# Recurrent layer pair on one core: tail over two chunk times, fewer spread banks, more product banks

## The reference, cut to what matters

```python
xn = layernorm(x)
s = mamba_block(xn)              # below
g = silu(fp4_down(silu(fp4_gate(xn)) * fp4_up(xn)))   # blockwise 4-bit quantised inputs and weights
x = x + s * g
xn = layernorm(x)
s = attention(xn)                # 16 heads of 16, over the 2 sequences at each token
g = silu(three blocks of h + linear(gelu(layernorm(linear(h)))))   # with bias; low rank part folded into weights
x = x + s * g

def mamba_block(x):
    u = layernorm(x) * g1 + b1
    xi, z = u @ in_proj          # 512 each
    xc = silu(causal_conv(xi, 4 taps per channel) + conv_b)
    dt, Bm, Cm = split(xc @ x_proj)
    dt = softplus(dt @ dt_proj + b)
    h[t] = exp(dt[t] * A) * h[t-1] + dt[t] * Bm[t] * xc[t]     # 512 channels x 16 states
    y[t] = sum over states of h[t] * Cm[t], plus D * xc[t]
    x = x + (y * silu(z)) @ out_proj
    return x + gelu(layernorm(x) @ w1 + b1) @ w2 + b2
```

## Time and profile before

| | us |
|---|---|
| median of 3 runs | 2985.43 |
| lowest, highest | 2978.42, 2988.9 |
| the profiled execution | 2981.44 |
| its span | 2979.3 |
| mean granted clock of PE, of full speed | 0.782 |

### The profile page before, as it was taken

How to read it: one execution, slowest core, us unless ns; L and a number is a source line. 1 busy time by engine, 2 the same in 40 slices (tenths; PEclk the granted TensorE clock), 3 DMA queues, 4 the chain that set the end, 5 groups by cost and what they waited for, 6 DMA issues and landing times.

```text
span 2979.3 us, 28883 instructions
## 1 busy us (share of the span) xinstructions
PE 1925.2 (65%) x7760; PEld 1465.3 (49%) x7760; DVE 1937.7 (65%) x2306; ACT 1486.6 (50%) x2992; POOL 1526.0 (51%) x1329
## 2 busy tenths in 40 slices
PE   0555857577685757667575776857667575765766
PEld 0333646455464545546454554645455464544644
DVE  2367767766676776667677666766666676766642
ACT  0255646446463544646464474645547364654532
POOL 1167555656355565536556463655556364555431
PEclk9956878778787878877787787878778786877877
DMA  5000000000000000000000000000000000000000
GB/s 143 4 11 1 1 1 11 1 12 1 11 1 0 12 1 11 1 12 1 1 11 1 12 1 11 1 0 12 0 11 1 12 1 0 11 1 8 1 8 4
DMA packets 31524, 25.55 MB, mean 9 GB/s; under 512 B 12038, under 2 KB 30278, under 8 KB 31318
## 3 DMA queue, kind: packets, MB, share of 16 engines
q1 hardware_dynamic: 31318, 23.23, 2.8%
HBM read 19.03 MB, written 4.19 MB: 8 GB/s over the span
## 4 chain that ended last, share of the span: by engine, by line
PE 23%; POOL 21%; issue 19%; ACT 19%; DVE 12%; POOLq 1%; ACTq 1%; DVEq 0%; DMA 0%
PE bank L488 9%; POOL drive L905 5%; ACT decay L723 4%; ACT L723 4%; PE bank L481 3%; DVE drive L1030 3%; PE bank L647 3%; POOL xd L1003 3%; PE bank L519 2%; POOL t_sm L929 2%; POOL wide L1008 2%; DVE dt L1221 2%; PE bank L603 2%; PE bank L537 1%; POOL drive L904 1%
## 5 line engine op out<-in xcount | busy, mean ns | idle before, releaser
L1030 DVE TENSOR_TENSOR_SCAN drive<-decay,drive 128x1032 f32<-128x1032 f32 x256 | 606.0, 2367 | 278.4 <-POOL drive L905 259.7
L905 POOL TENSOR_TENSOR drive<-wx,bc_sb 128x1024 f32<-128x1024 f32 x256 | 614.7, 2401 | 0.0
L904 POOL TENSOR_TENSOR drive<-carry,zero 128x8 f32<-128x8 f32 x256 | 124.9, 488 | 862.0 <-ACT carry L732 784.8
L655 PE MATMUL y_ps<-ident,decay 128*128 128x128 f32 x2048 | 353.8, 330 | 285.1 <-DVE decay L1035 279.3
L655 PEld LDWEIGHTS y_ps<-ident,decay 128*128 128x128 f32 x2048 | 307.6, 174 | 340.7 <-DVE decay L1035 292.8
L723 ACT ACTIVATE decay<-dt,aneg 128x256 f32<-128x256 f32 x1024 | 435.3, 499 | 1.5
L1035 DVE TENSOR_TENSOR decay<-drive,bc_ps 128x1024 f32<-128x1024 f32 x256 | 312.5, 1221 | 8.8
L664 PE MATMUL bc_ps<-bc,pick 64*128 64x256 f32 x512 | 157.2, 395 | 159.2 <-DVE decay L1035 159.1
L488 PE MATMUL bank<-w_l,op_b 128*128 128x256 f32 x384 | 177.2, 642 | 77.3 <-ACT op_b L813 45.7
L664 PEld LDWEIGHTS bc_ps<-bc,pick 64*128 64x128 f32 x512 | 96.9, 236 | 218.2 <-DVE decay L1035 167.4
L927 POOL TENSOR_TENSOR t_sm<-t_mv,epsc 128x2 f32<-128x2 f32 x80 | 49.3, 617 | 269.9 <-DVE t_mv L1046 269.9
(11 more groups left out here) (199 smaller groups left out, 4380.4 us busy)
## 6 DMA issues: line engine op xcount, KB each, us to landing
x_t<-in_L_attn_x_dram SPq DMA_DIRECT2D x16, 256.0 KB, 2.9
x<-in_L_attn_x_dram SPq DMA_DIRECT2D x16, 256.0 KB, 2.9
out_dram<-s SPq DMA_DIRECT2D x16, 256.0 KB, 2.2
w_f<-in_L_attn_ffn_w_dram SPq DMA_DIRECT2D x2, 1024.0 KB
q_raw<-in_L_ffn_qweights_dram SPq DMA_DIRECT2D x1, 1536.0 KB
w_in<-in_L_attn_in_proj_w_dram SPq DMA_DIRECT2D x1, 1024.0 KB
b_l<-in_L_ffn_biases_dram SPq DMA_DIRECT2D x1, 768.0 KB
qkv_raw<-attn_in_proj_weight_dram SPq DMA_DIRECT2D x1, 768.0 KB
```

The source lines that it names most:

```text
L655: last = t.matmul(y_ps[j][:, g * P:(g + 1) * P], src(g, j), ident[:, :], start=(first and g == 0), stop=stop, is_transpose=True, skip_grou ...
L904: g_.tensor_tensor(d[:, :, 0], carry[:, n, :], zero8[:, :], ALU.add).then_inc(S["drive_ready"], 1)
L905: g_.tensor_tensor(d[:, :, 1:SEG].rearrange("p (g b) t -> p g b t", b=B), wx[par][:, :, :].rearrange("p g (b t) -> p g b t", b=B), bc_sb[n ...
L1030: v.tensor_tensor_scan(drv[:, :, :].rearrange("p s t -> p (s t)"), dec[:, :, :].rearrange("p s t -> p (s t)"), drv[:, :, :].rearrange("p s ...
```

## The change

- The tail is cut in A (out_proj and ffn) and B (attention, first block, first half of the second) for chunk c-1, and C (the rest) for chunk c-2. `x1` and `h` are doubled. There is one more period at the end.
- M now holds all quantised work of chunk c; its input is quantised at the end of the period before, and it has its own operand `xq_t`.
- Two banks `bc_ps` for the spread of B and C, four `bank` for dense products, in one order over all periods (`ORDER`, `BANK`, `EARLIER`). A product waits for the reader of the product four before it.
- ACT copies B and C to `bc_sb`, and h*C reads C from there. The copy of n waits for h*C of n-2; the spread of n waits for the copy of n-2 and no longer for an h*C.
- The convolution is made by PE: weights times each tap (`w_tap`, made in the preparation) on shifted columns of `u_t`, which keeps the last three columns of the chunk before; ACT's silu reads PSUM.
- y is summed by two products of 512 columns with the identity as weights, channels on partitions; D*x is a product with a diagonal. y needs no transposing before out_proj, and z is made with channels on partitions.
- Biases are one more product from rows of `b_rows` or `b_qkv` into the same bank.
- A tail norm is: DVE statistics and an add, one POOL power (`root`), two DVE passes in a later slot (`norm_apply`); three of them read PSUM.
- The loop is gone: every period is written out by the program that builds the kernel, and waits are for constants.

```diff
+USES = {
+    "A": [("op", "dve"), ("u2T", "act")] + [(f"f1{_m}", "act") for _m in range(4)] + [("f2", "dve")],
+    "B": [("xn1T", "act"), ("b0a", "dve"), ("qkv0", "dve"), ("qkv1", "dve"), ("qkv2", "act"), ("qkv3", "act"),
+          ("b0T", "act"), ("b0b", "dve"), ("ctxT", "act"), ("h1T", "act"), ("ao", "dve"), ("b1a", "dve")],
+    "C": [("b1T", "act"), ("b1b", "dve"), ("h2T", "act"), ("b2a", "dve"), ("b2T", "act"), ("b2b", "dve")],
+    "F": [("uT", "act"), ("xi0", "act"), ("xi1", "act"), ("z0", "act"), ("z1", "act"), ("xp", "dve"),
+          ("dt0", "act"), ("dt1", "act")],
+    "M": [("xqT", "act")] + [(f"{_n}{_j}{_h}", "act" if _n == "g" else "dve")
+                             for _j in range(2) for _n in "gu" for _h in range(2)]
+         + [(f"hqT{_k}", "act") for _k in range(3)] + [("dn", "act")],
+}
+OWN = {"A": -1, "B": -1, "C": -2, "M": 0, "F": 1}
+NBANK = 4
+NSPREAD = 2
+
+
+PE_SLOT = {
+    1: [("C", "b1T"), ("A", "op")],
+    2: [("M", "xqT"), ("C", "b1b")],
+    3: [("M", "g00"), ("M", "g01"), ("M", "u00"), ("M", "u01"), ("A", "u2T"), ("C", "h2T")],
+    4: [("M", "g10"), ("M", "g11"), ("M", "u10"), ("M", "u11"), ("A", "f10"), ("A", "f11"), ("C", "b2a")],
+    5: [("A", "f12"), ("A", "f13"), ("F", "uT")],
+    6: [("A", "f2"), ("C", "b2T"), ("F", "xi0")],
+    7: [("C", "b2b"), ("F", "xi1")],
+    8: [("F", "z0"), ("F", "z1")],
+    9: [("B", "xn1T"), ("F", "xp")],
+    10: [("B", "b0a"), ("B", "qkv0"), ("B", "qkv1"), ("B", "qkv2"), ("B", "qkv3"),
+         ("M", "hqT0"), ("M", "hqT1"), ("M", "hqT2")],
+    11: [("M", "dn"), ("F", "dt0"), ("F", "dt1")],
+    12: [("B", "b0T")],
+    13: [("B", "b0b")],
+    14: [("B", "ctxT"), ("B", "h1T")],
+    15: [("B", "ao"), ("B", "b1a")],
+}
+PERIODS = range(-1, NC + 2)
...
+ORDER = [(_c + OWN[_g], _g, _n) for _c in PERIODS for _s in range(NS) for _g, _n in PE_SLOT.get(_s, [])
+         if there(_c + OWN[_g])]
+BANK = {_key: _k % NBANK for _k, _key in enumerate(ORDER)}
+EARLIER = {_key: ORDER[_k - NBANK] for _k, _key in enumerate(ORDER) if _k >= NBANK}
...
+        y_ps = [ctx.enter_context(nc.psum_tensor(f"y_ps{j}", [P, 2 * TOK], F32)) for j in range(2)]
+        bc_ps = [ctx.enter_context(nc.psum_tensor(f"bc_ps{k}", [P, 2, TOK], F32)) for k in range(NSPREAD)]
         bank = [ctx.enter_context(nc.psum_tensor(f"bank{k}", [P, 512], F32)) for k in range(NBANK)]
...
+                (xi_raw[:, :, :], in_proj_w[:, 0:DI].rearrange("(k p) n -> p k n", p=P)),
+                (w_z[:, :, :], in_proj_w[:, DI:2 * DI].rearrange("(k p) n -> p k n", p=P)),
+                (cw_raw[:, :, :], conv_w.rearrange("d o t -> o d t").to_broadcast([P, DI, NTAP])),
...
+            def tokens(dst, lhs, rhs, kp, group, row=None):
 
                 for j in range(B):
                     for k in range(kp):
-                        last = t.matmul(dst[:, j * cols:(j + 1) * cols], lhs(k, j), rhs(k),
-                                        start=(k == 0 and j == 0), stop=(k == kp - 1), skip_group_check=True)
+                        last = t.matmul(dst[:, j * D:(j + 1) * D], lhs(k, j), rhs(k),
+                                        start=(k == 0 and j == 0), stop=(row is None and k == kp - 1),
+                                        skip_group_check=True)
+                if row is not None:
+                    last = t.matmul(dst[:, 0:B * D], ident[0:NROW, row:row + 1].to_broadcast([NROW, P]),
+                                    b_rows[:, None, :].to_broadcast([NROW, B, D]), start=False, stop=True,
+                                    skip_group_check=True)
                 last.then_inc(S["pe_" + group], 1)
...
+                elif name[:2] == "xi":
+                    m = int(name[2])
+                    pe.wait_ge(*emptied("F", fc, "uT"))
+                    for a in range(2):
+                        for tap in range(NTAP):
+                            for k in range(KD):
+                                last = t.matmul(dst[:, a * TOK:(a + 1) * TOK],
+                                                w_tap[:, tap, k, (2 * m + a) * P:(2 * m + a + 1) * P],
+                                                u_t[:, k, :, tap:tap + TC],
+                                                start=(k == 0 and tap == 0 and a == 0),
+                                                stop=(k == KD - 1 and tap == NTAP - 1), skip_group_check=True)
+                    last.then_inc(S["pe_F"], 1)
...
-            def sum_y(src, first, stop):
-
-                for j in range(B):
-                    for g in range(DG):
-                        last = t.matmul(y_ps[j][:, g * P:(g + 1) * P], src(g, j), ident[:, :],
-                                        start=(first and g == 0), stop=stop, is_transpose=True, skip_group_check=True)
+            def sum_y(hc, stop):
+
+                for m in range(2):
+                    last = t.matmul(y_ps[m][:, :], ident[:, :], hc[:, 4 * m:4 * m + 4, 1:SEG],
+                                    start=False, stop=stop, skip_group_check=True)
                 last.then_inc(S["y_summed"], 1)
 
-            def broadcast(chunk, par, n):
-
-                before = max(m for m in range(n - NS, n) if SPREAD[m % NS] == SPREAD[n])
-                pe.wait_ge(S["hc_done"], value(chunk, "hc_done", before + 1))
+            def skip_y():
+
+                for g in range(DG):
+                    last = t.matmul(y_ps[g // 2][:, (g % 2) * TOK:(g % 2 + 1) * TOK], d_diag[:, g, :], xc[:, g, :],
+                                    start=(g % 2 == 0), stop=False, skip_group_check=True)
+                last.then_inc(S["y_summed"], 1)
+
+            def broadcast(chunk, n):
+
+                pe.wait_ge(S["bc_sbuf"], value(chunk, "bc_sbuf", n - 1))
+                dst = spread(chunk, n)
                 for k, r in enumerate((n, NS + n)):
-                    last = t.matmul(bc_ps[SPREAD[n]][:, k, :], pick[:, r:r + 1].to_broadcast([64, P]), bc[par][:, :],
+                    last = t.matmul(dst[:, k, :], pick[:, r:r + 1].to_broadcast([64, P]), bc[chunk % 2][:, :],
                                     start=(k == 0), stop=True, skip_group_check=True)
                 last.then_inc(S["bc_spread"], 1)
...
+                act.wait_ge(S["hc_done"], value(chunk, "hc_done", n - 1))
+                a_.activation(bc_sb[n % 2][:, :, :], spread(chunk, n)[:, :, :], ACT.Copy).then_inc(S["bc_sbuf"], 1)
                 if n >= 4:
                     act.wait_ge(S["y_summed"], value(chunk, "y_summed", n - 2))
...
+                        act.wait_ge(S["u_saved"], value(fc - 1, "u_saved", 1))
+                        for k in range(KD):
+                            last = a_.activation(u_now[:, k, :, :],
+                                                 dense("F", fc, "uT")[:, k * TOK:(k + 1) * TOK]
+                                                 .rearrange("p (b t) -> p b t", b=B),
+                                                 ACT.Identity, scale=g1c[:, k:k + 1], bias=b1c[:, k:k + 1])
+                        last.then_inc(S["act_F"], 1)
+                    if s in (6, 7):
+                        m = s - 6
+                        act.wait_ge(*filled("F", fc, f"xi{m}"))
+                        two(lambda k: xc[:, 2 * m + k, :], dense("F", fc, f"xi{m}"), ACT.Silu, lambda k: 1.0,
+                            lambda k: cb[:, 2 * m + k:2 * m + k + 1], "F")
+                    if s == 8:
...
+            def root(name, of, chunk):
+
+                pool.wait_ge(S[of], value(chunk, of, 5))
+                g_.tensor_tensor(rstd[:, :], veps[:, :], mhalf[:, :], ALU.pow).then_inc(S[name], 1)
...
-                dve.wait_ge(S["bc_spread"], value(c, "bc_spread", n + 1))
                 v.tensor_tensor(dec[:, :, 1:SEG].rearrange("p (g b) t -> p g b t", b=B),
                                 drv[:, :, 1:SEG].rearrange("p (g b) t -> p g b t", b=B),
-                                bc_ps[SPREAD[n]][:, 1, :].rearrange("p (b t) -> p b t", b=B)[:, None, :, :]
+                                bc_sb[n % 2][:, 1, :].rearrange("p (b t) -> p b t", b=B)[:, None, :, :]
                                 .to_broadcast([P, DG, B, TC]), ALU.mult).then_inc(S["hc_done"], 1)
...
+            def norm_stats(src, name, chunk):
+
+                stats(src, t_st, t_mv, name, chunk)
+                dve.wait_ge(S[name], value(chunk, name, 4))
+                v.tensor_scalar(veps[:, :], t_mv[:, :, 1], EPS, None, ALU.add).then_inc(S[name], 1)
+
+            def norm_apply(dst, src, name, chunk, done):
+
+                dve.wait_ge(S[name], value(chunk, name, 1))
+                for j in range(B):
+                    last = v.tensor_scalar(dst[:, j, :], src[:, j, :], t_mv[:, j, 0:1], rstd[:, j:j + 1],
+                                           ALU.subtract, ALU.mult)
+                last.then_inc(S[done], 1)
...
+                if s == 1:
+                    dve.wait_ge(*filled("A", tc, "op"))
+                    dve.wait_ge(S["f_norm"], value(tc, "f_norm", 4))
```

(30 more changed lines are left out.)

## The result

The changed kernel takes 2996.53 us (median of 20 runs, 2983.18 to 3008.45) against 2983.63 (20 runs) for the kernel before: 1.0038 times as long, 95% interval 1.0025 to 1.0051. It is slower by a hair, where the prediction said 2755. The profiled execution has a span of 2995.4 us.

The account below looks back on a forecast made before the run. No engine is full, so waits set the time. Start 178, first chunk 128, second 151, thirteen of 157 (2041), last scanning period 140 and tail 115 make a span of 2753, plus 2: 2755 us; range 2555 to 3000.

Parts of the forecast that it names:

- The walk of 16 slots: Steady chunk, from h*C of state 3 onward, following what is late next through the queues: 157 us where 174 are now.
- warm paces for all of PE's work: PE in a steady chunk: work priced at high-clock times, 132 us after the change, four-matrix products at 1.8 us.
- Its own sign for the PE terms: PE: sum of y of 1.8 us, busy near 135 to 145 us a chunk, clock above 0.85.
- The second rival: PE's clock stays as it is: work in slots 3 to 11 takes 17 us more, 174 a chunk, about 2990; chance 0.08.
- The price of C in SBUF: h*C: +1.4 us in the five or six states after slot 12 that DVE and POOL bound, nothing elsewhere.
- The first rival: Turns of DVE and POOL at the port pair decide: 181 us a chunk, 3091 in all, slower; chance 0.15.
- attention and residual 3.1: Walk between h*C after state 13 and the three 1.22 us passes: attention and residual take 3.1 us.
- Engine sums: Busy time of a steady chunk: PE 132 us of warm work, DVE 110, POOL some 73, ACT near 98.
- Waits costed at nothing: ACT's copy waiting for h*C, the spread waiting for ACT's copy, SP's load order and the unrolled program: no cost.
- The waits only move: ACT, in order with 24 table loads, still holds up carries: 11 us more DVE idle, 168 a chunk, 2909; chance 0.11.
- The longest gaps: Sign for the walk: longest gaps between scans in slots 6 to 9 and 12 to 13.

Follow-up runs that it names:

- fill_qkv: Changed kernel with zero-weight filler products on PE in slot 10 alone, 3 before the third and 3 before the fourth qkv product: 2936.2 us (0.9837).
- keep_warm: Changed kernel with zero-weight filler products in front of PE's waits in seven places, 3 and 1 of them in slot 10: 2917.5 us (0.9761).
- psum33_warm: Changed kernel with C read from PSUM, three spread and three product banks, and zero-weight fillers before PE's waits: 2866.1 us (0.9579).
- no_pool_softplus: Changed kernel with POOL's two softplus passes of 1024 elements cut to 8 elements, values not the reference's: 2947.3 us (0.9874).
- szs_warm: Changed kernel with softplus Exp and Ln in slot 12, z products in slots 12 and 13, convolution silu a slot later, and fillers: 2766.0 us (0.9266).
- the three moves: Changed kernel with, each alone, softplus Exp and Ln in slot 12 (2903.8 us), convolution silu a slot later (2960.2), z products in slots 12 and 13 (2958.2).

## Why the prediction was wrong

The walk of 16 slots can be set beside the timelines, by the ends that it named (us; means of the thirteen steady chunks).

| stretch of the walk, ends with | walk | after | fill_qkv | keep_warm | psum33_warm | no_pool_softplus | szs_warm |
|---|---|---|---|---|---|---|---|
| h*C of state 5 | 20.0 | 18.4 | 18.4 | 18.4 | 19.4 | 18.4 | 18.4 |
| product xi1 | 31.0 | 31.7 | 31.7 | 31.7 | 31.7 | 31.7 | 31.7 |
| ACT's copy of xn1T | 14.6 | 13.0 | 13.0 | 13.0 | 12.6 | 13.0 | 8.3 |
| ACT's last copy of hqT | 15.4 | 21.4 | 18.5 | 20.1 | 22.1 | 21.4 | 19.2 |
| decay of state 13 | 19.0 | 20.8 | 19.8 | 19.9 | 19.6 | 20.8 | 15.1 |
| DVE's product wx | 16.0 | 20.1 | 20.1 | 20.1 | 19.5 | 17.1 | 20.1 |
| b1a statistics and copy | 13.0 | 16.0 | 16.3 | 13.8 | 13.8 | 15.8 | 13.8 |
| h*C of state 3 | 28.0 | 32.0 | 31.2 | 30.2 | 26.3 | 31.8 | 30.2 |
| chunk | 157 | 173.3 | 168.9 | 167.2 | 165.0 | 170.1 | 156.8 |

**The step that failed: warm paces for all of PE's work.** The walk's first three stretches, where PE is at 1.00, came out 2.5 us shorter than forecast. The other five are 18.8 us longer. In them PE waits, the clock falls, and its work is on the path. The fillers before all these waits (`keep_warm`) take 6.1 us off a steady chunk. If the larger gain of the two filler kernels is taken in each stretch (2.9, 1.0, 2.2 and 1.8 us in the fourth, fifth, seventh and eighth), it is 7.8; no one kernel has all of these. The prediction had 3.78 against 1.8 us for such a product in its own rows and a clock of 0.77, and still said that the busiest stretches are warm; they are, but it priced the idle ones warm too. Its own sign for the PE terms, a clock above 0.85, was met (0.855) and could not tell. The second rival, "the clock stays as it is", gave 174 a chunk and 2990 and had 0.08. Its time is nearly exact, but partly by luck: its mechanism is some two fifths of the miss, and it put the slow work in slots 3 to 11, where it was in 11 to 15 and 0. Its chance was too small. The range from 2555 to 3000 holds the measured time only by this rival's end of it.

**Turns.** The price of C in SBUF was near: +1.4 in five or six states, measured 6.3 us in five states of a steady chunk, and longest case 3.36. It is a mean of 0.3 to 2.1, and two of the five states are not after slot 12. The walk says that it holds these 7 to 8 us, but its terms show a turn plainly in state 15 alone (6.1); state 0 stands at 3.5 and took 5.6 (2.30 and 3.34). With fillers, C in PSUM takes 3.9 us off the eighth stretch and 0.6 off the sixth, so a part of the price is in the miss; which part, the terms don't tell. The first rival (181 a chunk, with 7 us in which neither DVE nor POOL works) is refuted: both are idle together for 33 us a chunk, and by taking C out of SBUF 78 us are gained, not 240. The rule cited ("SBUF — State Buffer", "Who interferes with whom" in the Trainium skill) agrees with these lines: with C in PSUM no h*C took over 1.222 us.

The walk also had every scan at 2.31 us. In the changed kernel those of states 3, 6, 8, 10, 12 and 13 took 2.75 to 3.41 as a mean, each begun beside a pass of POOL: 42.2 us a chunk for all sixteen, 37.8 before. And it left out that short steps with two SBUF inputs wait as long as large ones: "attention and residual 3.1" has a step of 0.18 us that took 2.37 and one that took 2.04. POOL's softplus passes are 3.0 of the 4.1 us by which that stretch is over: 0.75 through the scan, 2.2 through the first of these steps. Another 8 us of the 18.8 no run takes apart. C in SBUF, bank waits of the qkv products, the long scan of state 10 and further short turns (the add of two elements) lie there. That these are all of it is not shown.

**Engine sums.** PE: 147.2 us a chunk at a clock of 0.85, just over the 135 to 145 that were given; the four passes of a sum of y follow each other by 0.43 us, 1.72 (1.8 forecast), xi 13.8 for 64 passes (14.3). DVE 122.2, not 110: 6.3 of it are longer h*C and 4.4 longer scans; the rest wasn't taken apart. POOL 86, not 73: its five powers take 9.7 us a chunk where 5.7 were forecast, and six small passes (front norm and attention) 10.8 where the same ones took 2.7 before. ACT 95.3 (98 forecast, though 92.0 and the terms given make 95.5 or less), with 24 table loads as counted. DVE idles for 52 us, not 30; the forecast's own 157 less 110 would have been 47.

**Waits costed at nothing.** ACT's copy waits for h*C of two states before for 20.6 us a chunk; the price of this wait by itself wasn't measured. The spread, also costed at nothing, waits for ACT's copy of two states before once, for 2.9 us, in slot 12. Not only qkv3 waits for a bank: qkv2 does too, for 1.33 us, and these two small waits cost the 60 us that the fillers of slot 10 bring. What the unrolled program brought by itself no run shows: the thirteen steady chunks take 173.3 us each where they took 174.1. The start took 8 and the first chunk 8 us more than forecast, the second 14. With C in PSUM the first chunk took 126.7 us, with three and three banks and C in SBUF 138.0.

**"The waits only move"** (fourth rival, 168 a chunk, ACT holds up the carries) names a part as well. Its figure is near the 170 us of several kernels above, and moving ACT's steps in its queue gains 185 us of 2996 together with z. But these waits were in the walk, near their size (19.0 forecast, 20.8 measured for the stretch with softplus). They are what could be improved, not what was missed. The longest gaps were said to lie in slots 6 to 9 and 12 to 13. Slots 7, 8, 12 and 13 are among the longest; 11 (17.1) and 4 (14.0) were missed, and 6 and 9 (9.5 and 6.1) are short.

With C in PSUM and fillers, in the changed kernel's own order, a chunk takes 165.0 us. The forecast plus the lost bank (23 / 16) is 158.4, and some 151 if the five turns of 1.4 us that are gone there are taken off: between 7 and 14 us a chunk are still missed. The direction hung on the small sums: C in PSUM, the fillers or any of the three moves alone makes the change faster than the kernel before.

## What to carry to other kernels

A walk along in-order queues can be exact where an engine is full and still be 10% off in the end: price each of PE's stretches at the clock that stretch will have. Here it was low in slots 11 to 15 and 0, where PE waits for others. Where different queues bound different slots, a saved microsecond is worth a fraction. Fractions may add (C in PSUM and the clock), shrink (fillers on top of the moves) or grow (the later silu on top of the others), so measure them together. Look first for a step that waits for this slot's product while the next state's short steps stand behind it, and put it a slot later.

## What the runs showed of the hardware

- Work added to PE made the kernel faster: 1622 more matmul passes and 197 us more PE busy time, 79 us less in all (2388.3 to 2585.8 busy, clock 0.855 to 0.952).
- The clock fell 0.6 us after 1.33 us of idle time, with 92 us at the high level before it. Three filler products ahead of this wait and three ahead of the next one, of 0.69 us, held it at 1.00 through slot 11 in all thirteen steady chunks; three and one did so in four of them.
- Chunks settle at a few lengths. In the changed kernel ten of thirteen steady ones took 174.0 or 174.1 us and the others 170.7 or 170.8; with three product banks and C in SBUF all thirteen lie between 173.6 and 174.1, without table loads eleven are 163.8 or 163.9. Slot 11 takes about 17.5 us where its clock is 0.61, 15.6 where it is 0.78 (the chunks of 170.7), and 14.2 with fillers, at 1.00. Why just these lengths is open, and so is whether they hide a part of what an edit saves inside a chunk. Two kernels alternate between two lengths, so a mean must take neighbouring chunks: with fillers in seven places mostly 165.4 and 168.8, with C in PSUM 168.2 and 173.1.
- A DVE step of 32 elements (0.18 us) takes 2.37 us beside POOL's 3 us pass, and ends as that pass does: it waits for the end of the other engine's instruction, whatever its own size. A scan begun beside a POOL pass takes 2.75 to 3.41 us instead of 2.31; for five of six states the excess is about what was left of that pass (0.6 to 1.2 us), for state 13 it is 0.75 us beside a pass of 3.64.
- A change of function on ACT costs 1.283 us each time (all 138 loads at L726), with no further gap in front: 2.5 us idle before all of them.
